# Reordering the opening of cross attention in a decoder block: value products among the maxima, part-by-part query moves, GpSimd's bias additions moved

## The reference

```
x = layernorm(x + self_attention(x))          # latent projections, rotary parts added, softmax over 1024 keys
x = layernorm(x + cross_attention(x, ctx))    # 154 context keys, masked
x = layernorm(x + moe(x))                     # 8 experts, each takes its top 256 tokens of a batch
```

## Time and profile before

| | us |
|---|---|
| median of 3 runs (lowest, highest) | 1693.08 (1692.09, 1695.22) |
| the profiled execution: its time, its span | 1693.32, 1691.5 |
| TensorE busy in that span | 1527.0 (90%) |
| VectorE busy | 1230.9 (73%) |
| ScalarE busy | 864.4 (51%) |
| GpSimd busy | 433.2 (26%) |

### The profile page before, as it was taken

The page is one execution under the profiler, slowest core; times in us unless marked ns, Lnnn a source line. Parts: engine busy times, 40 slices in busy tenths (PEclk is TensorE's granted clock), DMA queues, the critical chain, the costliest instruction groups (busy, mean ns, idle before and its releaser), DMA issues. The chain is left out here.

```text
span 1691.5 us, 24385 instructions
## 1 busy us (share of the span) xinstructions
PE 1527.0 (90%) x8366; PEld 700.0 (41%) x8366; DVE 1230.9 (73%) x2543; ACT 864.4 (51%) x1626; POOL 433.2 (26%) x547
## 2 busy tenths in 40 slices
PE   7499999988999988989999889899987888999995
PEld 2222323534222244342232443422224436888875
DVE  5488873788888877878888689788885765664454
ACT  3167775544677744447777435377773341111111
POOL 5140000521300006113000160130000213666763
PEclk9799999999999999899999999999998898999998
DMA  6500000453200004532000054410000224555595
GB/s 181 152 19 1 2 3 28 119 149 85 79 2 2 30 0 132 135 90 74 1 2 30 0 150 117 120 45 2 1 1 23 55 70 129 111 113 117 99 271 134
DMA packets 101432, 121.52 MB, mean 72 GB/s; under 512 B 20412, under 2 KB 90812, under 8 KB 100156
## 3 DMA queue, kind: packets, MB, share of 16 engines
q1 hardware_dynamic: 86396, 98.95, 20.3%
q0 software_dynamic: 13920, 19.68, 6.7%
q10 hardware_dynamic: 992, 1.32, 0.2%
HBM read 68.76 MB, written 31.09 MB: 59 GB/s over the span
## 5 line engine op out<-in xcount | busy, mean ns | idle before, releaser
L1225 ACT ACTIVATE pT<-banks 128x512 f32<-128x512 f32 x1184 | 650.1, 600 | 273.1 <-PE banks L2099 150.3
L1545 DVE TENSOR_REDUCE nmf<-banks 128x1 f32<-128x1024 f32 x512 | 601.1, 1219 | 114.9 <-PE banks L2014 114.0
L2099 PE MATMUL banks<-qst,kst 99*128 99x512 bf16 x1024 | 342.4, 385 | 8.5 <-DVE nmf L1545 6.3
L2014 PE MATMUL banks<-kst,qst 96*128 96x512 bf16 x1024 | 308.6, 383 | 27.5 <-DMA qst<-oT 21.8
L2131 PE MATMUL banks<-pT,V 128*32 128x512 f32 x2048 | 274.4, 607 | 16.4 <-ACT oT L1213 12.3
L2099 PEld LDWEIGHTS banks<-qst,kst 99*128 99x128 bf16 x1024 | 95.6, 97 | 284.4 <-ACT pT L1225 185.9
L938 POOL CAST nmp<-nmf 128x16 bf16<-128x16 f32 x64 | 12.6, 197 | 715.5 <-issue 600.5
L2014 PEld LDWEIGHTS banks<-kst,qst 96*128 96x128 bf16 x1024 | 95.5, 98 | 140.7 <-issue 30.8
L1395 ACT ACTIVATE kst<-banks 128x512 f32<-128x512 f32 x64 | 38.1, 597 | 206.6 <-PE banks L2459 206.6
L992 POOL DMA_INDIRECT acc_rows<-kst,tok_s x62 | 100.6, 1622 | 41.9 <-issue 16.8
L1805 DVE TENSOR_SCALAR kst<-banks,gate 128x256 f32<-128x256 f32 x64 | 28.0, 479 | 93.2 <-PE banks L2472 93.2
(11 more groups left out here) (255 smaller groups left out, 2097.7 us busy)
## 6 DMA issues: line engine op xcount, KB each, us to landing
qst<-q_parts SPq DMA_DIRECT2D x36, 256.0 KB, 4.8
kst<-k_parts SPq DMA_DIRECT2D x36, 256.0 KB, 7.4
qst<-in_w SPq DMA_DIRECT2D x16, 512.0 KB, 5.2
qxs<-in_w SPq DMA_DIRECT2D x16, 512.0 KB, 5.3
qst<-oT SPq DMA_DIRECT2D x60, 128.0 KB, 2.5
qxs<-oT SPq DMA_DIRECT2D x48, 128.0 KB, 2.5
xb<-in_x SPq DMA_DIRECT2D x4, 1024.0 KB, 6.4
x_rows<-z SPq DMA_DIRECT2D x4, 1024.0 KB, 8.4
```

The lines of the kernel that those rows point to most:

```text
L1225: act.activation(pT[:, n % RING_P, :], PS[:, banks[what, n], :], ACT.Exp, scale=scale).then_inc(s_ex, 1)
L1545: dve.tensor_reduce(nmf[:, m % 2, j, t:t + 1], scores.rearrange("p a n -> p (a n)"), AX.X, ALU.max, negate=True).then_inc(s_smu, 1)
L2014: ins = pe.matmul(pair[:, half, :], qst[0:KQ, h, t * P:(t + 1) * P], kst[0:KQ, h, half * N:(half + 1) * N], start=True, stop=True)
L2099: ins = pe.matmul(ps, kst[0:KM, head, kc * P:(kc + 1) * P], qst[0:KM, head, cols], start=True, stop=True)
```

## The change

The value products (`v` 0 to 3) leave the place after the key products and go among the maxima of cross attention, after units 9, 11, 13 and 15, all in bank 7; ScalarE copies each there. Query chunks 2 and 3 are made right after the keys, in banks 6 and 7, once VectorE has taken the sixth key product, and ScalarE writes their parts ahead of and between those of key pieces 6 and 7. SyncE moves them part by part, ahead of the stores of pieces 4 and 5, and the row of group 0 comes after them. GpSimd's `after_layernorm` becomes two halves, after the splits of groups 0 and 1, in all four batches; `bias_values` goes behind the split of group 7.

```diff
+LEAD_BANKS = (6, 7, 7, 7, 7, 7)
+VALUES_AFTER = (9, 11, 13, 15)
...
-EACH = Plan(LATENTS[:1] + OUT_SELF + LATENTS[1:] + HALF_Q + TURNED + HALF_X + HALF_Q + KEYS + VALUES + HALF_X,
+EACH = Plan(LATENTS[:1] + OUT_SELF + LATENTS[1:] + HALF_Q + TURNED + HALF_X + HALF_Q + KEYS + HALF_X + VALUES,
...
+    if step[0] == "smax" and step[1] in VALUES_AFTER:
+        ORDER_AHEAD.append(("values", VALUES_AFTER.index(step[1])))
...
-                    for i in range(2, 6):
-                        store_piece((b + 1, i))
-                    load_cross(2)
+                    store_piece((b + 1, 2))
+                    store_piece((b + 1, 3))
+                    load_cross_part(2, 0)
+                    load_cross_part(3, 0)
+                    store_piece((b + 1, 4))
+                    for part in (1, 2):
+                        load_cross_part(2, part)
+                        load_cross_part(3, part)
+                    store_piece((b + 1, 5))
                     load_minus_max(b, NG, cross_rows(0))
-                    load_cross(3)
                     load_minus_max(b, NG + 1, cross_rows(1))
...
                 split_max(b, SM_SELF, NG, cross, range(1))
+                after_layernorm(b, 0)
                 split_max(b, SM_SELF, NG, cross, range(1, 2))
-                after_layernorm(b)
-                split_max(b, SM_SELF, NG, cross, range(2, 4))
-                if more:
-                    bias_values(b + 1)
-                split_max(b, SM_SELF, NG, cross, range(4, NG))
+                after_layernorm(b, 1)
+                split_max(b, SM_SELF, NG, cross, range(2, NG))
...
                 if more:
+                    bias_values(b + 1)
                     split_max(b + 1, 0, 0, own, range(1))
...
-                    values(at)
                     cross_part(at, b, 2, 0)
+                    cross_part(at, b, 3, 0)
                     part1(at, (b + 1, 6))
+                    cross_part(at, b, 2, 1)
                     part1(at, (b + 1, 7))
-                    cross_part(at, b, 3, 0)
+                    cross_part(at, b, 3, 1)
+                    cross_part(at, b, 2, 2)
+                    cross_part(at, b, 3, 2)
                     part2((b + 1, 6))
                     part2((b + 1, 7))
-                    for part in (1, 2):
-                        cross_part(at, b, 2, part)
-                        cross_part(at, b, 3, part)
...
+                        if cross:
+                            wait_taken(at, "A", at.nth("v", n))
                         value(at, n)
...
+                        if order is ORDER_AHEAD and n == 0:
+                            wait_taken(at, "A", at.nth("v", 3) + 1)
...
-                    values(at)
+                    wait_taken(at, "D", at.nth("k", 5) + 1)
                     cross_query(2)
                     cross_query(3)
```

More of the change, by code:

```diff
@@ L123, in bank @@
             return LATE_BANK
+        if self.plan is EACH and self.nth("qx", 2) <= idx <= self.nth("v", 3):
+            return LEAD_BANKS[idx - self.nth("qx", 2)]
         if self.plan is EACH and self.plan.items[idx][0] == "x2T":
@@ L964, in bias_values, with after_layernorm @@
                                    .to_broadcast([P, T, H, HD]), ALU.add).then_inc(s_vb, 1)
-            def after_layernorm(b):
+            def after_layernorm(b, half):
+                tiles = slice(half * T // 2, (half + 1) * T // 2)
                 pool.wait_ge(s_ln, b * 2 * T + T)
-                pool.tensor_tensor(xb[:, :, :], z[:, :, :], brow[:, 3:4, :].to_broadcast([P, T, D]),
-                                   ALU.add).then_inc(s_xb, 1)
+                ins = pool.tensor_tensor(xb[:, tiles, :], z[:, tiles, :],
+                                         brow[:, 3:4, :].to_broadcast([P, T // 2, D]), ALU.add)
+                link(ins) if half == 0 else ins.then_inc(s_xb, 1)
             def mask_bias(b):
@@ L1157, in part2 @@
                 act.activation(middle, rest[:, n % 2, 0:cols], ACT.Copy).then_inc(s_p3, 1)
-            def values(at):
-                for k in range(4):
-                    value(at, k)
             def value(at, k):
@@ L1237, in attention @@
                     elif what == "values":
-                        value(FIRST_AT, n)
+                        value(at or FIRST_AT, n)
                     elif what == "context":
@@ L1313, in rest_of_batch @@
                 attention(b, ST_SELF, NG, ST_CROSS, ORDER_AHEAD if more else ORDER_LAST,
-                          BANKS_AHEAD if more else BANKS_CROSS, SCALE_CROSS, NUMBER[(b + 1, 7) if more else (b, 8)] + 1)
+                          BANKS_AHEAD if more else BANKS_CROSS, SCALE_CROSS, NUMBER[(b + 1, 7) if more else (b, 8)] + 1, at)
                 if more:
@@ L2072, in attention @@
                     elif what == "values":
-                        if n == 0:
+                        if n == 0 and not cross:
                             pe.wait_ge(s_wb, 80)
+                        if cross:
+                            wait_taken(at, "A", at.nth("v", n))
                         value(at, n)
@@ L2123, in attention @@
                             pe.wait_ge(s_ave, b * 2 * NG + (NG if cross else 0) + g)
-                        if order is ORDER_NEXT and n == 0:
+                        if order is ORDER_AHEAD and n == 0:
+                            wait_taken(at, "A", at.nth("v", 3) + 1)
+                        elif order is ORDER_NEXT and n == 0:
                             taken_upto(at, at.nth("lg") + 1)
@@ L2349, in rest_of_batch @@
                 if more:
-                    taken_upto(at, at.nth("v", 3) + 1)
+                    taken_upto(at, at.nth("qx", 2))
                 else:
```

## The result

| | before | after |
|---|---|---|
| median of 5 runs each (lowest, highest), us | 1692.09 (1689.22, 1695.22) | 1705.91 (1704.19, 1711.35) |
| profiled execution: time, span, us | 1693.32, 1691.5 | 1704.69, 1702.9 |
| TensorE, VectorE, GpSimd busy in the span, us | 1527.0, 1230.9, 433.2 | 1531.1, 1239.7, 433.7 |

The ratio is 1.0089, 95% interval [1.0075, 1.0103]. The forecast was 1699.5, slower, range 1690 to 1705: the direction and its main cause came as predicted, the time is 6.4 us above the forecast. The forecast stood on a median of 1693.08 from three runs, where five give 1692.09. As a growth it was 6.6 us, and the medians grew by 13.8, the profiled spans by 11.4. VectorE's busy time grew by 8.8 us although it executes the same instructions: that is the first thing to look at.

The account below looks back on a forecast made before the run. The prediction took VectorE's chain and SyncE's queue of loads to bound the first own maximum, VectorE having no slack thereafter. Its terms, -2.0 + 8.7 + 1.0 - 1.1 = +6.6 us, gave 1699.5 us, range 1690 to 1705.

Parts of the forecast that it names:

- The opening: After the key products: VectorE's wait before unit 4 falls from 3.3 us to about 0.5, the gain lost at unit 8.
- Values among the maxima: In cross attention VectorE waits 0.4 us for each moved value product, 1.6 in all, cancelled by a wait removed before unit 16.
- The wait before unit 16: VectorE's 1.31 us wait in the first opening, from GpSimd's long addition to xb; halving that addition takes it away.
- T: SyncE's issue of the next queries, 29.4 us after the key products end; with the second batch's extra 0.57, sum -2.0 us.
- rival B: TensorE's clock falls among the values too, delaying the next queries' issue one more us per batch: 1703 us, chance 0.12.
- The addition to V: Behind group 7, GpSimd's addition holds VectorE's division after the first own maximum, 2.9 us in three batches: +8.7 us.
- Rival A: No exclusion between GpSimd's addition to V and VectorE's division: 1690 us, chance 0.23.
- C: Group 7's split comes early enough that the addition ends before the division; opening gains nothing: 1692 to 1694, chance 0.11.
- The clock behind the stall: TensorE, idle during the held division, may return at the lower clock: 0 to 1.5 us each, 0.3 taken, +1.0 us.
- Last batch: Only the halved addition to xb bears on it: nearly all of 1.16 us before unit 16 goes, -1.1 us.

Follow-up runs that it names:

- v_only: The kernel before with only the addition to V moved behind group 7's split: ratio 1.0086 to the kernel before.
- v_back: The changed kernel with the addition to V put back behind group 3's split, amid the cross maxima: ratio 1.0003 to the kernel before.
- v_gap: The changed kernel with the addition to V moved behind own group 0's split, where GpSimd stands idle: ratio 0.9999 to the kernel before.
- v_quarters: The changed kernel with the addition to V, still behind group 7, made in four instructions: ratio 1.0012 to the kernel before.
- value_early: The changed kernel with the first value product put into TensorE's wait ahead of turn 0: ratio 1.0038 to the kernel before.
- one_input: The changed kernel, addition to V behind own group 0's split, a one-input GpSimd multiplication by 1.0 in its old place: ratio 1.0057 to the kernel before.
- xb_only: The kernel before with only GpSimd's addition to xb halved, behind the splits of cross groups 0 and 1: ratio 0.9992 to the kernel before.
- parts_only: The kernel before with only the new order of query and key parts on SyncE and ScalarE: ratio 0.9986 to the kernel before.
- parts_xb: The kernel before with the new parts' order and the halved addition to xb: ratio 0.9964 to the kernel before.

## Why the prediction was wrong in size

- **The opening: handed back at unit 8.** Right in all three batches: 0.41 us before unit 4, 2.19 to 2.75 before unit 8, GpSimd's last piece subtraction at 330.96 (predicted near 332), unit 8 at 333.13 (333.6 to 334.2), TensorE's wait for the sixth key product 1.97 us (2.2).
- **Values among the maxima, 0.4 us each.** Near where the clock stays (0.40, 0.82, 0.41 in the first batch), wrong in two of three batches, where the first cost 2.02. The wait before unit 16, which was to cancel them and to go in all four batches, went in the last one alone: 0.6 us of it is left in the other three (1.31, 1.73 and 1.16 before).
- **T, sum -2.0 us: this step failed.** T moved by -1.40, +0.61 and +1.84, together +1.1 us, where the prediction had -1.05, -0.63 and +0.23. O came 0.4 us sooner after T over the three batches, so that the term is +0.6 where -2.0 stood. The prediction had the 2 us wait ahead of turn 0 in its own sum, and two times for the row of group 1, with the clock up and with it down among the values. It took one between them, and gave rival B, the fall, a chance of 0.12. The fall came in two batches of three, and cost more than B's 1 us: T lies 1.2 and 1.6 us behind the forecast there, at 30.64 and 31.01, above the prediction's own bound of 30.4. Over the five kernels that pair this opening with late values the wait of 2.06 to 2.08 us stands 15 times ahead of turn 0. The granted clock stayed at 1.00 over turn 0 and the values in 4 of them. It fell in 11, and in each of these the first value product took 1.71 to 2.00 us against 1.07. By these counts the fall was the likely case.
- **The addition to V, +8.7 us.** Right: 8.5 in the changed kernel, 9.3 in v_only, gone in v_back and v_gap, and 0.5 in v_quarters. Rival A, no exclusion, and C, the addition done in time, are out.
- **The clock behind the stall, +1.0, bounded at 1.5 a batch: mis-sized.** In the twelve stalls of four kernels (changed, v_only, value_early, one_input) O to E grew by 19.3 us beyond the divisions' own lengths, 1.6 each, and by 3.4 in the changed kernel. It was nothing in one batch and 4.2 in the worst (v_only, the second). TensorE waited 1.7 to 2.6 us, and then ran at 0.50 for 3 to 10 us in 11 of the 12. The prediction took half of one low stretch of 3 us as the most, and 0.3 us a batch as the term.
- **Last batch, -1.1.** The wait before unit 16 went: the first masked maximum came 1.2 us sooner after M (13.97 against 15.18), and 0.9 in xb_only. The whole stretch M to E shrank by 2.3, but from first masked maximum to E it scatters by 4 us between kernels whose last batches are alike, so that what goes beyond 1.2 is not shown to come from the change.

The sum by what was measured, counted as the prediction counts: the opening +0.6, divisions 8.5, behind them 3.4, last batch -2.3, everything else 1.2: the span's 11.4. Against the predicted 6.6 the opening is 2.6 off and the clock behind the stall 2.4. The 1.2 elsewhere, for which there was no term, and the last batch's -1.2 cancel. The medians grew by 2.4 us more than the profiled pair. Without that, or with either of the two misses less, the time would have been inside the range.

## What to carry to other kernels

The long GpSimd addition of this kernel was free beside reductions of PSUM (v_gap, 0.9999) and dear ahead of a VectorE instruction with two SBUF inputs (0.43 us became 3.04 to 3.64). Place it in a gap that holds none, or cut it in pieces no longer than you can afford to wait.

A wait of 2 us on TensorE is not only 2 us: behind a stall it cost 1.6 us more on average, and up to 4.2. Before work is moved behind such a wait, price it at the lower clock. What runs there at half speed must have slack of its own, as the maxima had (a wait of 0.35 us) and the values had not (2.02). Filling the wait with a piece of the moved work kept the clock up over turn 0 and the values in 8 of 9 openings.

An edit that gains in one setting can lose in another, as the parts' order did: it makes a wait, and whether that matters depends on the work that another edit puts behind it. Run each alone and both together.

## What the runs showed that I had not expected

The division is let through at another moment than GpSimd's row ends: 4.46 us after the start of an addition of 4.17 us, the division's own 0.43 included, but only 3.94 us after the start of a multiplication of 5.39 us, in all three batches (1042.62 + 3.13 - 1041.81 in the third). So the "whole instruction" of the prediction can't be read off the recorded length of that row, and why is open.

The same wait of TensorE (2.06 to 2.08 us, ahead of the same instruction) came with the upper clock in 4 openings of the five kernels and with the lower in 11, within one execution too (first batch against second and third). With the six openings of parts_only and parts_xb, which have the same wait and the lower clock each time, it is 4 and 17. These rows say how often, not what decides.
